# Causal attention of a two-layer post-norm model on one core: layer 1 goes by halves of the queries

## What is computed

```python
def _L1_attn_ref(x, W_qkv, b_qkv, W_out, b_out):     # 16 heads of 16, causal
    qkv = x @ W_qkv.T + b_qkv
    ...
    scores = jnp.einsum('bnqd,bnkd->bnqk', q, k) * scale
    scores = jnp.where(causal, -jnp.inf, scores)
    attn = jax.nn.softmax(scores, axis=-1)
    ...
    return out @ W_out.T + b_out
def _L1_ffn_ref(...):                                # 256 -> 1024 -> 256, 4-bit weights and low-rank parts
    y1 = x1 @ w_up + b_up + x1 @ w_up_lora_a @ w_up_lora_b
    return relu(y1) @ w_down + b_down + relu(y1) @ w_down_lora_a @ w_down_lora_b
```

## Time and profile before

| | us |
|---|---|
| median of 3 runs | 880.75 (878.85 to 885.21) |
| the profiled execution, its own time | 880.45 |
| its span, first to last instruction | 878.4 |
| TensorE busy | 780.9 (89%) |
| VectorE busy | 455.7 (52%) |
| ScalarE busy | 359.3 (41%) |
| GpSimd busy | 97.7 (11%) |

### The profile page before, as it was taken

One profiled execution on the slowest core, in us unless ns is written; L12 is line 12 of the kernel. 1 busy time (PEld: TensorE's weight loads), 2 busy tenths in 40 slices (PEclk: granted clock), 3 DMA queues, 4 the chain that ended last, 5 costly groups with the idle time before them and its releaser, 6 DMA issues. The chain is left out here.

```text
span 878.4 us, 11506 instructions
## 1 busy us (share of the span) xinstructions
PE 780.9 (89%) x3907; PEld 412.9 (47%) x3908; DVE 455.7 (52%) x1213; ACT 359.3 (41%) x565; POOL 97.7 (11%) x111
## 2 busy tenths in 40 slices
PE   5599999999998999999997677879898899989886
PEld 3222434444335566666655334324454445533675
DVE  2733654464435622222235895786855675662443
ACT  3388865784871111111124114444422543146130
POOL 0000000000000011111641101222100101011000
PEclk9689999999999999999989799989999999989999
DMA  6558117006026061111124880003600180000000
GB/s 210 147 195 244 62 43 210 1 24 180 1 83 205 13 182 43 48 42 46 37 63 138 233 250 4 2 14 119 181 1 2 63 233 18 2 1 25 13 12 25
DMA packets 51581, 75.01 MB, mean 85 GB/s; under 512 B 7606, under 2 KB 44762, under 8 KB 49226
## 3 DMA queue, kind: packets, MB, share of 16 engines
q1 hardware_dynamic: 49660, 69.26, 26.2%
q0 software_dynamic: 1872, 5.11, 2.1%
HBM read 46.57 MB, written 27.66 MB: 85 GB/s over the span
## 5 line engine op out<-in xcount | busy, mean ns | idle before, releaser
L616 PE MATMUL ps<-arena 128*128 128x256 f32 (+5 forms) x1084 | 329.2, 452 | 22.8 <-DVE arena L1217 4.5
L616 PEld LDWEIGHTS ps<-arena 128*128 128x128 f32 (+1 forms) x1084 | 201.8, 196 | 112.3 <-issue 71.2
L922 ACT ACTIVATE arena<-ps 128x1024 f32<-128x1024 f32 x128 | 124.2, 1027 | 34.3 <-PE ps L658 34.1
L1017 ACT ACTIVATE arena<-ps 128x1024 f32<-128x1024 f32 (+3 forms) x128 | 82.6, 702 | 109.7 <-PE ps L855 109.6
L1378 DVE TENSOR_REDUCE arena<-ps 128x1 f32<-128x512 f32 (+3 forms) x176 | 101.4, 635 | 33.0 <-PE ps L833 32.2
L723 PE MATMUL ps<-arena 128*128 x184 | 86.5, 593 | 0.6 <-DVE arena L1114 0.6
L658 PE MATMUL ps<-arena 96*128 96x512 bf16 x256 | 72.2, 394 | 7.1 <-DMA arena<-q_stacks_dram 4.3
L831 PE MATMUL ps<-arena 96*128 96x128 bf16 (+3 forms) x256 | 65.0, 311 | 14.3 <-DVE arena L1378 8.8
L1465 POOL TENSOR_SCALAR_AFFINE_SELECT arena<-arena 128x512 f32<-128x512 f32 x64 | 42.3, 662 | 274.0 <-ACT arena L1017 274.0
L672 PE MATMUL ps<-arena 128*32 128x512 f32 x512 | 70.2, 615 | 2.9 <-DVE arena L1160 2.7
L1424 POOL DMA_INDIRECT arena<-xs_dram,arena x23 | 21.9, 953 | 404.7 <-DVE arena L1284 302.8
(11 more groups left out here) (145 smaller groups left out, 682.6 us busy)
## 6 DMA issues: line engine op xcount, KB each, us to landing
arena<-stacks_dram SPq DMA_DIRECT2D x16, 768.0 KB, 6.2
arena<-in_gate_up_proj SPq DMA_DIRECT2D x8, 1024.0 KB, 9.4
arena<-q_stacks_dram SPq DMA_DIRECT2D x8, 768.0 KB, 5.9
stacks_dram<-arena SPq DMA_DIRECT2D x16, 384.0 KB, 3.2
arena<-in_down_proj SPq DMA_DIRECT2D x8, 512.0 KB, 8.6
stacks_dram<-arena SPq DMA_DIRECT2D x16, 256.0 KB, 3.5
q_stacks_dram<-arena SPq DMA_DIRECT2D x8, 384.0 KB, 4.1
yg_dram<-arena SPq DMA_DIRECT2D x23, 128.0 KB, 1.7
```

The source lines that it names most:

```text
L616: last = nc.tensor.matmul(dst[0:rows, lo:hi], a, w, start=(n == 0), stop=(n == len(pairs) - 1))
L922: nc.scalar.activation(probs[:, 2 * p:2 * p + 2, :], ps[:, 2 * p:2 * p + 2, :], ACT.Exp)\
L1017: nc.scalar.activation(cprobs[:, i % 2, 2 * p:2 * p + 2, P * kt:S], ps[:, 2 * p:2 * p + 2, P * kt:S], ACT.Exp).then_inc(exp_done[p], 1)
```

## The change

The queries of a batch now go in two halves of 256, in 12 steps. Steps 0 to 3 are the first half's, one for each group of four heads, with both its tiles of keys; steps 4 to 11 are the second half's, two for each group (key tiles 0 and 1, then 2 and 3). Each step has two key tiles and so two matmuls a head for the scores and two quadruples for the product; 8 of 12 steps have diagonals. Output is turned after steps 1, 3, 7 and 11, for two groups of one half at a time.

What follows the halves: the 44 maxima are ordered by halves (12 for the first, 32 for the second), each half has its own `cM`, rows and semaphore; the projection of the first half, `cP0`, stands in step 5 of the same batch, and that of the second in the next batch's step 1, where the statistics of both halves and the norm now stand too; the last batch's first half has `cN0` and its eight up-projection steps inside the attention. The gathers of all batches are issued at the start: those of batches 0 and 1 into two buffers, of batches 2 and 3 added to x by the DMA itself.

```diff
+MAXES = [(qt, h, 4 // (qt + 1) if qt < 2 else 1) for half in range(2) for heads in range(2)
+         for qt in (2 * half, 2 * half + 1)
+         for h in range(NH // 2 * heads, NH // 2 * (heads + 1), 4 // (qt + 1) if qt < 2 else 1)]
+MAXES0 = sum(qt < 2 for qt, h, n in MAXES)
+GROUPS1 = (2, 4, 8, 12)
+def step1(i):
+    if i < HG:
+        return 0, i, (0, 1)
+    return 1, (i - HG) // 2, (0, 1) if i % 2 == 0 else (2, 3)
+def blocks1(i):
+    half, hg, kts = step1(i)
+    blocks, at = [], 0
+    for kt in kts:
+        lo = max(P * kt, C * half)
+        hi = C * (half + 1)
+        blocks.append((kt, lo, hi, at))
+        at += hi - lo
+    return blocks, at
+def has_diagonal(i):
+    half, hg, kts = step1(i)
+    return kts[0] // 2 == half
...
-C_SECOND = """-cF3 +cX0 | -cP0 +cX1 +cQ0 | +cK0 -cP1 +cQ1 | +cK1 +cQ2 | .cF0 +cQ3 +cK2 =cO0 +cK3 | +cV0 +cV1 =cO1
...
+C_SECOND = """-cF3 +cX0 .m .m .m .m | -cP1 +cX1 +cQ0 .m .m .m .m | .cF0 .m .m .m .m .m .m .cM1 +cK0 +cQ1 -cN0 -cN1
...
+| .cF2 -cD0 +m +m +m +m +m +m | -cD1 +m +m +m +m +m +m +cM0 | -cD2 >cL0 +m +m +m +m +m +m +m +m | -cD3 >cL1 +m +m +m +m +m +m +m +m +m +m"""
+C_THIRD = C_SECOND
...
 (TensorE: scores, product, projection)
-                        last = nc.tensor.matmul(ps[:, g, P * kt:S], ck_stack[0:STACK + 2, b % 2, h, cols(kt)],
-                                                cq_stack[0:STACK + 2, b % 2, h, P * kt:S], start=True, stop=True)
+                        for kt, lo, hi, at in blocks1(i)[0]:
+                            last = nc.tensor.matmul(ps[:, g, at:at + hi - lo], ck_stack[0:STACK + 2, b % 2, h, cols(kt)],
+                                                    cq_stack[0:STACK + 2, b % 2, h, lo:hi], start=True, stop=True)
...
+                    if i in (0,) + GROUPS1:
+                        pe.wait_ge(o_evac, HG * (B + b) + ((0,) + GROUPS1).index(i))
+                    if has_diagonal(i):
+                        pe.wait_ge(masked, 2 * HG * b + (i + 1 if half == 0 else HG + hg + 1))
...
-                    pe.wait_ge(cat_ready, 2 * (b + 1))
+                    pe.wait_ge(cat_ready, 4 * b + 2 * (i + 1))
...
 (VectorE: norm of a whole batch)
-                stats(i, rows[:, 2 * i:2 * i + 2, :])
                 if halves:
+                    stats(i, rows[:, 2 * i:2 * i + 2, :])
                     normalise(dst[:, 2 * i:2 * i + 2, :], rows[:, 2 * i:2 * i + 2, :], 2 * i, 2 * i + 2, done_sem, 2 * b + i + 1)
                 elif i:
+                    for half in range(2):
+                        stats(half, rows[:, 2 * half:2 * half + 2, :])
                     normalise(dst, rows, 0, NT, done_sem, 2 * b + 2)
...
 (VectorE: cF)
-                    v.wait_ge(pv_done, head0 * B + headc * b + NT * (i + 1))
-                    nc.vector.transpose(co_sb[:, i, :], ps[:, 4, :]).then_inc(o_evac, 1)
+                    half, pair = i // 2, i % 2
+                    v.wait_ge(pv_done, head0 * B + headc * b + GROUPS1[i])
+                    turned = co_sb[:, i, :]
+                    nc.vector.transpose(turned, ps[:, 4, :]).then_inc(o_evac, 1)
...
+                    nc.vector.transpose(c_a_t[:, pair, C * half:C * (half + 1)], rows).then_inc(cat_ready, 1)
...
 (GpSimd: gathers and select)
+                    if b < 2:
+                        nc.gpsimd.indirect_dma_start(out=yrow_of[b][:, t, :], out_offset=None, in_=yg_dram, in_offset=at)\
+                          .then_inc(gathered[b], 16)
+                    else:
+                        nc.gpsimd.indirect_dma_start(out=x_sb[:, NT * b + t, :], out_offset=None, in_=yg_dram, in_offset=at,
+                                                     compute_op=ALU.add).then_inc(gathered[b], 16)
...
+                    for p in range(2):
+                        pool.wait_ge(exp_done[p], k + 1)
+                        diag = cprobs[:, i % 2, 2 * p:2 * p + 2, :].rearrange("p g (u n) -> p g u n", u=2)[:, :, :, 0:P]
+                        last = nc.gpsimd.affine_select(out=diag, in_=diag, compare_op=ALU.is_ge, fill=0.0, base=0,
+                                                       pattern=[[0, 2], [0, 2], [1, P]], channel_multiplier=-1)
+                    last.then_inc(masked, 1)
```

More of the change, by code:

```diff
@@ L114, in expand, with attention_order @@
     return steps
-def attention_order(fills, name):
+def attention_order(fills, name, n, m):
     steps = []
-    last = B * NT * HG - 1
+    last = B * n - 1
     for b, fill in enumerate(fills):
-        m = [0]
-        *fill, rest = fill.split("|")
-        assert len(fill) == NT * HG and not rest.strip()
+        fill = fill.split("|")[:n]
+        assert len(fill) == n
         for i, names in enumerate(fill):
-            k = b * NT * HG + i
+            k = b * n + i
             if k == 0:
@@ L409, in post_ln_layers @@
         m_parts = sem("max_parts_ready")
-        s_m = sem("max_rows_loaded")
+        s_m = [sem(f"max_rows_loaded{h}") for h in range(2)]
         kones = sem("k_ones_ready")
```

155 lines of the change are left out of this document (80 added, 75 removed).

## The result

The changed kernel takes 905.87 us (median of four runs, 904.65 to 909.58) against 881.13: a ratio of 1.028 with a 95% interval of 1.025 to 1.031, slower. The forecast was 882.0, the range 866 to 895. The profiled execution took 905.06 us, with a span of 903.3.

A forecast was written before the change was run, and what follows sets the result against it. TensorE was taken to bound the middle, chains through VectorE and DMA both ends. Stages: -26.6 + 10.0 + 8.3 + 2.2 + 22.5 - 21.5 = -5.1 us; with 7 for the clock, +1.9 on 880.45 gives 882, range 866 to 895.

The forecast's parts named there:

- The clock: Half clock behind TensorE's gaps: 7 us added; as rival, each gap drops it, 16 us, 891 us, chance 0.2.
- a mean clock under 0.94 behind 512: Sign, behind 512 us on the timeline, that the forecast is wrong and the clock rival right.
- I take 7: About ten TensorE gaps; a 3.4 us half-clock stretch costs 1.7 where TensorE sets the pace, nothing where VectorE does.
- The batches: Layer 1's attention stages, batches 0 to 3: +10.0, +8.3, +2.2 and +22.5 us, with TensorE waiting for VectorE.
- the bound of 16: Upper bound of the clock's cost, from the skill's rule that every gap is paid: 16 us, time 891.
- the norm of batch 3: In batch 1, between a down-projection and ten maxima: TensorE waits 5.2 us.
- the projection's in batch 3: Norm in batch 3, without X and Q to fill it: 6 us of waiting.
- The start: Layer 1 until batch 0's first scores: 87.9 to 61.3 us, a gain of 26.6, first scores at 511.6.
- stacks 4 us late: Bound for the start: second half's stack reads landing 4 us later put first scores at 516, a gain of 22.
- The tail: Behind the last attention product: 55.2 to 33.7 us, a gain of 21.5.
- The ends win: Rival: waits in batches 1 to 3 don't get worse, the sum is -23.6 us, 857 us; chance 0.2.
- the start doesn't get shorter: Rival at the start: second half's stacks land 8 us later and maxima of heads 8 to 15 wait, 890 us; chance 0.1.

The follow-up runs named there:

- Experiment 9: Changed kernel with 840 idle matmuls put in 57 places, mostly where TensorE waits for VectorE: 891.60 us, ratio 1.012.
- experiment 16: Changed kernel with idle matmuls at nearly all the places of the 57-place run, but none at the three longest waits: 894.90 us, ratio 1.015.
- experiments 12: Changed kernel with idle matmuls (40, 64 and 64) at the three longest TensorE waits alone: 906.01 us, ratio 1.029.
- experiment 14: Changed kernel with idle matmuls in its waits, batch 3's norm four steps earlier and the adding gathers later: 886.25 us, ratio 1.007.
- experiment 13: Changed kernel with the adding gathers of batches 2 and 3 issued at batch 0's first attention steps instead of the start: 906.16 us, ratio 1.027.
- Experiment 7: Changed kernel with batch 3's first half of the last feed-forward put back behind the last attention product: 910.37 us, ratio 1.033.

## Why the prediction was wrong

Experiment 9 lets the 23 us of error (905.06 - 882.0 for the profiled execution) be split, since its batches hold no clock. Us per stage:

```
                        start  batch 0  batch 1  batch 2  batch 3  tail   sum
forecast, full clock     61.3     59.3    101.4     92.2     75.1  33.7  423.0
experiment 9             67.0     62.0    105.4     94.5     77.2  33.7  439.8
after                    66.3     63.4    111.3     98.0     80.6  33.4  453.0
```

- **The clock: 14, not 7.** In the four batches 353.3 - 339.1 is 14.2 us (14.3 by the medians of the whole kernel; start and tail of experiment 9 are 1.0 longer), 7 more than taken, and a lower bound. The prediction's own sign for it, a mean clock under 0.94 behind 512, is there: 1 - 32.2 / 386.7 = 0.917. It stood inside the bounds (0 to 16); the failing step is "I take 7". That was taken from a stretch of 3.4 us at half clock and from one gap of two that was followed by 1.00. The trace of before has more gaps, and two more stretches behind gaps of 2 to 3 us show what was missed:

```profile
585.70:592.50 6.80, 6.80 (x32) 2.29 (x31) 4.41 (x15) 4.07 (x6) 3.37 (x4) 0.50 0.13 37
784.20:790.50 6.30, 6.12 (x22) 3.09 (x23) 5.73 (x26) 2.28 (x4) 0.37 (x1) 0.50 0.00 0
```

  They last over 6 us, as the two shown after the result do, and in the first TensorE is busy throughout and VectorE is not. The cover by VectorE, which the prediction counted on, is real but partial: about two thirds of the loss behind the long waits, about half of that behind the short ones (experiment 16). The Trainium skill ("TensorE: Matmul & The Clock Gate", section "A second HAM failure mode: psum-queue depth-cycling") tells of brief idling between groups of matmuls that makes the clock swing and costs throughput. The batches agree with it: between 0.89 and 0.94, and 14.2 us dearer than at 1.00. That every gap is paid, the bound of 16 that I drew from it, comes nearer in size than my 7, but experiments 12 and 16 show that not every gap is.
- **The batches: +11 at full clock.** 2.7, 4.0, 2.3 and 2.1 more than the terms. The waits that were listed came: the norm of batch 3 was priced at 5.2 and TensorE waited 5.6 for it, that of batch 2 at 4.0 and it waited 3.4, the projection's in batch 3 at 6 and it waited 5.5. In experiment 14, where the norm of batch 3 stands elsewhere, batch 1 at full clock is 5.0 shorter. What is missing is spread evenly. For batch 2 of experiment 9 the timeline of TensorE, summed from start to start, says where it lies: products, transposes, scores and attention products take 63.7 us, where the terms have 62.7; maxima and rows, waits and idle matmuls together take 31.1, where the terms have 12.9 + 16.6. So the paces were about right (a record of 512 columns takes 0.43 us, as used; the recorded divisions are a little off, 3.67 / 8 is 0.46, 3.93 / 8 is 0.49, 3.08 / 5 is 0.62), and more of it is around the maxima. How much of that is the idle matmuls' own cost was not separated.
- **The start: +5.** 66.3 is the far bound that the prediction gave for stacks 4 us late ("516"). They were late: the last stack read was issued by 497.1 instead of 493, and where the adding gathers stand later it was 493.7 and the rows' transposes came 3.3 us earlier (experiment 13). The rest lies behind these transposes: from 509.06 to the first scores at 516.5 it took 7.4 us, where the two Q/K steps behind ScalarE have 2 x (1.72 + 1.27) = 6.0 in the prediction. That the stacks alone made the start late is not shown, since no run brought the first scores to 512.
- **The tail: right,** 33.4 for 33.7. Experiment 7 puts the price of half of that gain, in batch 3, at 6.8 where 7 to 8 was forecast.
- **The rivals.** "The ends win" was wrong: the waits came. "The clock" and "the start doesn't get shorter" were both right in kind. Each was priced alone, at 891 and 890, and the range, up to 895, reached hardly beyond one of them; they came together, with 11 us in the batches.

In sum the change took 43.4 us out of the two ends and put 68.3 into the batches: VectorE's work is the same (266.82 us instead of 267.63 in the six stages), but more of it now stands where TensorE waits for it, and behind these waits TensorE also runs at half clock.

## What to carry to other kernels

Two adverse rivals that can come true at once, here the clock and the late start, are not alternatives: price them together, and let the range reach there. A gap's clock costs more where the bounding engine has its own work behind the gap than where another engine paces what follows (here about half of the loss against a third), so look at what follows, not only at the gap's length. And lay all the gaps of a trace beside each other, not one for and one against. Before a reorder is believed, fill its waits with idle matmuls once: what comes back is the least that the clock cost.
